# Causal scores in two row halves of the TensorE array, with the batch loop written out

## The chip, the cores and the metric

The kernel runs on one core of one Trainium2 chip. The metric is the device time of one execution in microseconds (us). A change of about 0.2% is what a measurement of this kernel can tell from none. TensorE (PE) does matmuls, VectorE (DVE) reductions and elementwise work, ScalarE (ACT) exponentials and copies, GpSimd (POOL) masks, and SyncE (SP) starts the DMAs.

## What is computed

Two layers over eight sequences of 512 tokens with 128 channels. The change lies in one part of the last layer, grouped-query causal attention with 16 heads of 8 channels and 4 key/value heads:

```python
q = (x @ wq.T).reshape(B, S, N_HEADS, HEAD_DIM)
k = (x @ wk.T).reshape(B, S, N_KV_HEADS, HEAD_DIM)
v = (x @ wv.T).reshape(B, S, N_KV_HEADS, HEAD_DIM)
attn = jnp.einsum('bqhd,bkhd->bhqk', q, k) * scale
attn = jnp.where(causal, attn, -jnp.inf)
attn = jax.nn.softmax(attn, axis=-1)
out = jnp.einsum('bhqk,bkhd->bqhd', attn, v).reshape(B, S, C)
return out @ wo.T
```

Here B = 8, S = 512, N_HEADS = 16, HEAD_DIM = 8. Before it stand dilated attention, a ternary feed-forward layer and a gated attention; behind it a mixture of eight experts.

## The kernel before

Five phases follow each other, each closed by a barrier of all engines; names in the profile begin with a_, b_, c_, d_ and e_ by phase. The change touches the end of c_ (projections) and all of d_ (`causal_attention_phase`).

**Precision by stacking.** Queries and keys are fp32 values held as three bf16 parts. Six products of parts are stacked along the contraction, so that one head's scores contract over 6 x 8 = 48 rows (`ROWS`) in one bf16 matmul. Phase c_ stores these stacks in `q_stack` and `k_stack` (L832, L834) with one entry for each batch, and an entry for a batch 8 that does not exist, since the loop of d_ loads one batch too many.

**Two heads in one layout.** `Qs` holds head i of the first eight heads on rows 0 to 47 and head 8 + i on rows 48 to 95. `Ks` has a slot for each key head, with the key on the 48 rows of its own half and zeros on the other 48 (L1173), so that a matmul over 96 rows gives the score of one head alone. Six more rows hold the negated row maxima of both heads (three bf16 parts each) against rows of ones and zeros (L1174 to L1184).

**First scores** (`first`, tile `pS`): for a head, query tile q against keys 0 to 128(q+1), 512, 384, 256 and 128 wide, and behind each a 128 x 128 matmul of the identity with the triangle of -1e30. These are three fills (f = 0: 512; f = 1: 384; f = 2: 256 and 128), in two PSUM buffers by turns. DVE takes the maxima of each (`maxima`, L1197 to L1200). They are split into three parts, transposed (`rows`, tile `pM`) and sent by DMA into the last rows of `Qs`.

**Second scores** (`second`, tile `pT`): keys by queries, for head i and head 8 + i together, now over 102 rows with the maximum subtracted; widths 512, 384, then 256 and 128 in three units. ACT takes the exponential of a unit into `P` (L1276), POOL cuts the diagonal blocks (L1167).

**Values** (`values`, tile `pO`): fp32 matmuls over 128 keys, four heads in four groups of 32 columns of the array at once. `by_token` transposes the result into `pM`, DVE divides.

**Order.** I call the work on one pair of heads a round: three units, eight rounds a batch, 64 in all. PE's queue in a unit is the second scores of the batch at hand, two fills of first scores of a pair three rounds ahead, and one step of the values of earlier heads. The first 22 heads' fills stand alone ahead of the first round; I call this the lead-in. The batches run as 0, a hardware loop over (1, 2), (3, 4), (5, 6), and 7; in the loop, waits go through registers. Batch 7 has no fills; batch 6 still makes those of six heads of the batch that does not exist. A matmul's rows in the profile are written rows*columns: 96*128 is 96 rows of contraction by 128 columns of weights.

Of the kernel before, what the change touches and what calls it, by code (L numbers as in the profile page):

```python
# [17 lines left out]
DH, HEADS = 64, 16  # L18
# [17 lines left out]


def wait_alone(eng, sem, count, unit=1):


    if not isinstance(count, int):
        count = eng.to_reg(count)
        eng.wait_ge(sem, unit)
    eng.wait_ge(sem, count)
# [749 lines left out]
def projection_phase(nc, top, dram):  # L794

    with ExitStack() as ctx:
# [22 lines left out]
        with nc.Block() as block:  # L819

            @block.sync
            def _(sp):
                for k in range(CHUNKS):
# [4 lines left out]
                    for b in (0, 1, 1) if k == CHUNKS - 1 else (0, 1):  # L828
                        entry = 2 * k + b + (1 if n_stored[c] == 12 * (k // 2) + 12 else 0)
# [184 lines left out]
def causal_attention_phase(nc, top, dram):  # L1014
# [11 lines left out]
    with ExitStack() as ctx:  # L1026
        ph = Phase(nc, ctx, "d_")
        sm = ph.sems("zeros ones ones_from max_ones S S_max part1 rest1 part2 rest2 parts mT_psum mT ST P masked PV O_sb O_T rden O_tok")
# [6 lines left out]
        Ks = [ph.sb(f"Ks{c}", [128, KV4, S], BF16) for c in two]  # L1035
# [16 lines left out]
        ALL_ROWS = 2 * ROWS  # L1052
        WITH_MAX = ALL_ROWS + 6
# [3 lines left out]
        def wait(eng, sem, value):  # L1057

            if not isinstance(value, int) or value > 0:
                eng.wait_ge(sem, value)  # L1060

        def steps(eng, step):
# [12 lines left out]
        def others(n, m, c, ahead):  # L1075

            return (n + 1, m + c, 1 - c) if ahead == 1 else (n + 2, m + 1, c)

# [6 lines left out]
        def turns(n, pair, unit, at):  # L1085

            got = turn(pair, unit, at)
            ended = isinstance(n, int) and n == B
            if got is None or (got[0] == 0 and ended) or (got[0] == 1 and isinstance(n, int) and n == 0):
# [4 lines left out]
        everything = [(k, f) for k in range(HEADS) for f in range(3)]  # L1094
        SPLIT_AT = HEADS // 2 - LEAD
        parity = [0]

        def par(n):

            if isinstance(n, int):  # L1100
                parity[0] = n % 2
            else:
                parity[0] = 1 - parity[0]
            return parity[0]

        with nc.Block() as block:

            @block.sync
            def _(sp):
                def load_stack(b, c, u):  # L1110

                    for a in two:
                        rows = slice(ROWS * a, ROWS * a + ROWS)
                        sp.dma_start(Qs[c][rows, 4 * u:4 * u + 4, :], dram["q_load"](b, 8 * a + 4 * u, 4))\
                            .then_inc(stacks[c][u], 16)
                        sp.dma_start(Ks[c][rows, 2 * a + u:2 * a + u + 1, :], dram["k_load"](b, 2 * a + u, 1))\
# [5 lines left out]
                def max_rows(n, m, c):  # L1122
# [4 lines left out]
                    for a in two:  # L1127
                        at = ALL_ROWS + 3 * a
# [3 lines left out]
                def step(n, m, more):  # L1132
                    c = par(n)
                    if more:
# [3 lines left out]
                        if not (isinstance(n, int) and n + 2 > B):  # L1138
# [4 lines left out]
                        sp.wait_ge(sm["ST"], n * NT + NT)  # L1143
                        load_stack(n + 2, c, 1)

                sp.wait_ge(sm["zeros"], 2)
# [5 lines left out]
                steps(sp, step)  # L1152

                for a in two:
                    sp.wait_ge(stacks[0][a], 64 * (B // 2 + 1))

            @block.gpsimd
            def _(pool):
                def step(n, m, more):
                    par(n)  # L1160
                    for pair in range(HEADS // 2):
                        for unit in range(3):

                            wait_alone(pool, sm["P"], n * NT + 3 * pair + unit + 1)
# [10 lines left out]
                for c in two:  # L1175

                    pool.wait_ge(sm["ones"], c + 1)
                    for a in two:
                        view = Ks[c][ALL_ROWS:128, 2 * a:2 * a + 2, :]
                        nc.gpsimd.affine_select(out=view, in_=view, compare_op=ALU.is_ge, fill=0.0, base=-3 * a,  # L1180
                                                pattern=[[0, 2], [0, S]], channel_multiplier=1)\
                            .then_inc(sm["ones_from"], 1)
                        pool.wait_ge(sm["ones_from"], 2 * c + a + 1)
                        nc.gpsimd.affine_select(out=view, in_=view, compare_op=ALU.is_ge, fill=0.0, base=3 * a + 2,  # L1184
                                                pattern=[[0, 2], [0, S]], channel_multiplier=-1)\
                            .then_inc(sm["max_ones"], 1)
                steps(pool, step)

            @block.vector
            def _(dve):  # L1190
                def maxima(n, c, some):
                    for k, f in some:
                        h, fill = ORDER[k], 3 * k + f
# [39 lines left out]
                def step(n, m, more):  # L1233
                    c = par(n)
                    for pair in range(HEADS // 2):
                        if more and pair == SPLIT_AT:
                            split(n + 1, 1 - c)
                        for unit in range(3):
                            if more:
                                for ahead, k, f in fills(pair)[2 * unit:2 * unit + 2]:  # L1240
# [553 lines left out]
```

## Time and profile before

| | us |
|---|---|
| time, median of 3 runs | 903.62 |
| lowest and highest | 902.7, 904.41 |
| profiled execution, first to last instruction (span) | 900.7 |
| median less span | 2.9 |
| PE, DVE, ACT busy in the span | 643.0, 559.2, 403.3 |
| first matmul of d_ | at 406.78 |
| first exponential of batch 0, of batch 7 | at 456.22, at 719.64 |
| last exponential ends | at 746.45 |

The execution's own time is not listed apart from its span, so the span is set against the median. The view by slices cuts the span into 40 pieces of 22.5 us; each digit is the busy share of an engine in tenths, and PEclk is the granted TensorE clock in tenths, so 5 is 1.2 GHz and 9 is 2.4 GHz but for a rest. PE's busy time in the views counts a matmul from start to end, and each overlaps the next; how fast PE goes is read from the distances between starts. The end of a row of several matmuls is the end of its last. In the views that group by form, the columns are busy time, mean ns of one, and the idle time of the engine before them.

### The profile page before, as it was taken

Reading aid. Unit: us, or ns where it says so; the run is one execution under the profiler, and the core shown is the slowest. Engines: PE = TensorE matmul, PEld = TensorE weight load, DVE = VectorE, ACT = ScalarE, POOL = GpSimd, SP = SyncE. Lnnn points to the kernel's source line nnn. Section 1 sums busy time; section 2 is a strip of 40 time slices with the busy share of each in tenths; the row PEclk is TensorE's granted clock in tenths of the full one; section 3 lists DMA queues with packets and bytes.
Section 4 is the critical chain, followed back from the end, with each engine's and each line's share of the span. In section 5 each row is a group of like instructions: output and inputs, shape, how many; then the busy total and the mean of one; then the engine's idle time right before and its main releaser. Section 6 shows DMA issues by size and latency. Waiting matters only on the chain. (4 is left out here: it accounts for less than half of the span.)

```text
span 900.7 us, 13426 instructions
## 1 busy us (share of the span) xinstructions
PE 643.0 (71%) x4232; PEld 372.4 (41%) x4232; DVE 559.2 (62%) x1764; ACT 403.3 (45%) x794; POOL 222.6 (25%) x340
## 2 busy tenths in 40 slices
PE   0816338938754480708899999999999996789651
PEld 0816328117644270403244445454444523555320
DVE  5786974042463535307878878788787801478897
ACT  3682565410203424400046566665665673456541
POOL 1040310010003032333023333333333341134344
PEclk9957655555965665755579999999999997799896
DMA  6000000000000050253001111111011100000001
GB/s 236 1 0 1 1 1 1 0 2 1 1 1 0 1 175 0 70 168 81 17 1 49 36 37 30 33 40 42 26 38 33 36 13 1 0 1 1 23 24 47
DMA packets 19369, 28.61 MB, mean 32 GB/s; under 512 B 3310, under 2 KB 15102, under 8 KB 19146
## 3 DMA queue, kind: packets, MB, share of 16 engines
q1 hardware_dynamic: 18746, 25.94, 9.5%
q10 hardware_dynamic: 576, 2.10, 0.6%
q8 instruction: 23, 0.38, 0.2%
q14 instruction: 24, 0.20, 0.1%
HBM read 14.57 MB, written 11.35 MB: 29 GB/s over the span
## 5 line engine op out<-in xcount | busy, mean ns | idle before, releaser
L1276 ACT ACTIVATE d_P<-d_pT 128x768 f32<-128x768 f32 (+1 forms) x192 | 167.9, 881 | 110.8 <-PE d_pT L1293 110.8
L1197 DVE TENSOR_REDUCE d_mx<-d_pS 128x1 f32<-128x512 f32 (+1 forms) x268 | 160.9, 620 | 66.2 <-PE d_pS L1293 61.5
L1293 PE MATMUL d_pS<-d_Ks,d_Qs 96*128 96x512 bf16 (+3 forms) x536 | 150.4, 329 | 31.2 <-DMA d_Ks<-k_stack 25.1
L1167 POOL TENSOR_SCALAR_AFFINE_SELECT d_P<-d_P 128x256 f32<-128x256 f32 x256 | 101.0, 406 | 233.5 <-ACT d_P L1276 233.4
L1293 PE MATMUL d_pS<-mask_bf,ident_bf 128*128 128x128 bf16 x536 | 111.4, 236 | 0.0
L1293 PE MATMUL d_pT<-d_Qs,d_Ks 102*128 102x512 bf16 (+3 forms) x512 | 103.7, 305 | 1.1 <-ACT d_P L1276 0.5
L1293 PE MATMUL d_pO<-d_P,d_V 128*32 128x512 f32 (+3 forms) x1024 | 96.5, 451 | 1.9 <-POOL d_P L1167 1.5
L1293 PEld LDWEIGHTS d_pS<-d_Ks,d_Qs 96*128 96x128 bf16 x536 | 54.2, 101 | 100.1 <-DVE d_mx L1197 32.8
L1623 PE MATMUL e_PE<-gate_expT,e_oT 128*128 128x512 f32 x128 | 62.5, 634 | 11.0 <-DVE e_T L1519 10.4
L421 PE MATMUL a_PS<-ident,N 128*128 128x128 f32 x96 | 21.5, 403 | 63.5 <-ACT N L320 51.6
L1199 DVE TENSOR_REDUCE d_mx<-d_pS 128x1 f32<-128x256 f32 x134 | 56.3, 420 | 13.5 <-PE d_pS L1293 11.1
L1293 PEld LDWEIGHTS d_pT<-d_Qs,d_Ks 102*128 102x128 bf16 x512 | 35.7, 99 | 69.1 <-ACT d_P L1276 49.5
L1450 POOL TENSOR_TENSOR e_T<-e_T 128x512 f32<-128x512 f32 x32 | 40.7, 1279 | 93.5 <-DVE e_T L1519 77.9
L1293 PEld LDWEIGHTS d_pS<-mask_bf,ident_bf 128*128 128x128 bf16 x536 | 55.5, 104 | 7.1 <-issue 0.3
L1605 ACT ACTIVATE e_T<-e_PE,e_comb 128x128 f32<-128x128 f32 x128 | 34.7, 383 | 45.0 <-PE e_PE L1623 19.6
L421 PEld LDWEIGHTS a_PS<-ident,N 128*128 128x128 f32 x96 | 17.8, 212 | 66.7 <-ACT N L320 54.6
L415 POOL TENSOR_TENSOR X<-X,a_nT 128x1024 f32<-128x1024 f32 x8 | 19.5, 2433 | 92.0 <-ACT a_nT L320 92.0
L1623 PEld LDWEIGHTS e_PE<-gate_expT,e_oT 128*128 128x128 f32 x128 | 24.7, 205 | 40.8 <-issue 23.3
L990 PE MATMUL c_PA<-ident,c_a 128*128 128x128 f32 x32 | 7.9, 428 | 46.6 <-ACT c_a L950 46.6
L320 ACT ACTIVATE N<-X,a_nb,a_rs 128x128 f32<-128x128 f32 x96 | 37.8, 479 | 1.1 <-DVE a_nb L161 0.8
L1200 DVE TENSOR_REDUCE d_mx<-d_pS 128x1 f32<-128x128 f32 x134 | 37.6, 281 | 0.0
L1258 ACT ACTIVATE d_mT<-d_pM 48x512 bf16<-48x512 bf16 x8 | 4.7, 590 | 65.3 <-PE d_pM L1364 65.2
(256 smaller groups left out, 1056.8 us busy)
## 6 DMA issues: line engine op xcount, KB each, us to landing
d_Qs<-q_stack SPq DMA_DIRECT2D x36, 192.0 KB, 2.9
q_stack<-c_Qp SPq DMA_DIRECT2D x9, 384.0 KB, 2.7
q_stack<-c_Qp SPq DMA_DIRECT2D x9, 256.0 KB, 3.0
X<-in_x_dram ACTq DMA_DIRECT2D x4, 512.0 KB, 7.7
d_V<-V SPq DMA_DIRECT2D x8, 256.0 KB, 2.3
out_dram<-e_moe SPq DMA_DIRECT2D x4, 512.0 KB, 2.6
d_Ks<-k_stack SPq DMA_DIRECT2D x36, 48.0 KB, 2.8
w_qkvT<-in_w_qkvT_dram SPq DMA_DIRECT2D x1, 1536.0 KB
```

Of the source, the lines that this page charges most:

```text
L320: last = nc.scalar.activation(dst(t), src(t), ACT.Identity, bias=nb[c][:, t:t + 1], scale=rs[c][:, t:t + 1])
L415: nc.gpsimd.tensor_tensor(X[c][:, :, :], X[c][:, :, :], y[c][:, :, :], ALU.add).then_inc(sm[s + "_x"], 1)
L421: last = nc.tensor.transpose(dst(t), src(t), ident)
L1167: last = nc.gpsimd.affine_select(out=view, in_=view, compare_op=ALU.is_ge, fill=0.0, base=0, pattern=[[0, 2], [1, 128]], channel_multiplie ...
L1197: last = nc.vector.reduce_max(mx[c][:, 3 - f, h:h + 1], src[:, 0:512 - 128 * f], AX.X)
L1199: nc.vector.reduce_max(mx[c][:, 1, h:h + 1], src[:, 0:256], AX.X)
L1200: last = nc.vector.reduce_max(mx[c][:, 0, h:h + 1], src[:, 256:384], AX.X)
L1276: nc.scalar.activation(P[pair % 4][:, :, P_AT[unit]:P_AT[unit] + w], pT[(3 * pair + unit) % 2][:, :, 0:w], ACT.Exp, scale=float(HD4) ** -0 ...
L1293: return nc.tensor.matmul(out, lhsT, rhs, start=start, stop=stop)
L1450: nc.gpsimd.tensor_tensor(T[u % 4][:, 0:NE // 2, :], T[u % 4][:, 0:NE // 2, :], T[u % 4][:, NE // 2:NE, :], ALU.add).then_inc(sm["halved"], 1)
L1605: last = nc.scalar.activation(T[u % 4][:, e, :], PE_[1][:, e, :], ACT.Copy, scale=comb[u // CT][:, u % CT, e:e + 1])
L1623: return nc.tensor.matmul(out_, lhsT, rhs, start=start, stop=stop)
```

## The change

Each head of a pair gets its own half of the array: head i on rows 0 to 47, its three maxima on 48 to 50, and head 8 + i on rows 64 to 111 and 112 to 114. `Ks` needs two slots for four, no zeros, and one fill with ones. First scores contract over 48 rows, second scores over 51, and the two heads' second scores stand next to each other, width by width. The triangle is still a matmul over 128 rows. Fills go pair by pair: both heads' 512, both 384, both 256 and 128. The loop is written out, so batch 8 is neither stored, loaded nor scored, and no wait goes through a register.

```diff
-                    for b in (0, 1, 1) if k == CHUNKS - 1 else (0, 1):
-                        entry = 2 * k + b + (1 if n_stored[c] == 12 * (k // 2) + 12 else 0)
+                    for b in two:
+                        entry = 2 * k + b
...
-        Ks = [ph.sb(f"Ks{c}", [128, KV4, S], BF16) for c in two]
+        Ks = [ph.sb(f"Ks{c}", [128, KV4 // 2, S], BF16) for c in two]
...
-        ALL_ROWS = 2 * ROWS
-        WITH_MAX = ALL_ROWS + 6
+        WITH_MAX = ROWS + 3
+        half = lambda a, n: slice(64 * a, 64 * a + n)
...
-            step(0, 0, True)
-            with eng.Fori(0, B // 2 - 1) as i:
-                step(2 * i + 1, i, True)
-                step(2 * i + 2, i + 1, True)
-            step(B - 1, B // 2 - 1, False)
+            for n in range(B):
+                step(n, n // 2, n % 2, n < B - 1)
...
-            return [(1 + k // HEADS, k % HEADS, f) for k in places for f in range(3)]
+            return [(1 + k // HEADS, k % HEADS, f) for f in range(3) for k in places]
...
+            return [(ahead, k, f) for ahead, k, f in fills(pair)[2 * unit:2 * unit + 2] if n + ahead < B]
...
-                sp.wait_ge(sm["zeros"], 2)
+                sp.wait_ge(sm["ones"], 2)
...
-                    nc.gpsimd.memset(Ks[c][0:ALL_ROWS, :, :], 0.0).then_inc(sm["zeros"], 1)
-                    nc.gpsimd.memset(Ks[c][ALL_ROWS:128, :, :], 1.0).then_inc(sm["ones"], 1)
...
+                    nc.gpsimd.memset(Ks[c][:, :, :], 1.0).then_inc(sm["ones"], 1)
...
-                            mm(dst[:, at:at + w], Qs[c][0:ALL_ROWS, i, 128 * q:128 * q + 128],
-                               Ks[c][0:ALL_ROWS, h // 4, 0:w], True, False)
+                            mm(dst[:, at:at + w], Qs[c][half(a, ROWS), i, 128 * q:128 * q + 128],
+                               Ks[c][half(a, ROWS), h // 4 % 2, 0:w], True, False)
                             last = mm(dst[:, at + w - 128:at + w], top.ident_bf[:, :], top.mask_bf[:, :],
                                       False, True)
...
-                    for j in two:
-                        for kt, at in ((0, 0),) if unit == 0 else ((1, 0),) if unit == 1 else ((2, 0), (3, 256)):
-                            w = S - 128 * kt
-                            last = mm(dst[:, j, at:at + w], Ks[c][0:WITH_MAX, 2 * j + pair // 4,
+                    for kt, at in ((0, 0),) if unit == 0 else ((1, 0),) if unit == 1 else ((2, 0), (3, 256)):
+                        w = S - 128 * kt
+                        for j in two:
+                            last = mm(dst[:, j, at:at + w], Ks[c][half(j, WITH_MAX), pair // 4,
                                                                   128 * kt:128 * kt + 128],
-                                      Qs[c][0:WITH_MAX, pair, 128 * kt:S])
+                                      Qs[c][half(j, WITH_MAX), pair, 128 * kt:S])
```

PE's queue in the lead-in, the first fills of the first pair of heads. Before:

```order
L1293 MATMUL d_pS0<-d_Ks0,d_Qs0 128x512
L1293 MATMUL d_pS0<-mask_bf,ident_bf 128x128
L1293 MATMUL d_pS1<-d_Ks0,d_Qs0 128x384
L1293 MATMUL d_pS1<-mask_bf,ident_bf 128x128
L1293 MATMUL d_pS0<-d_Ks0,d_Qs0 128x256
```

The same place after the change:

```order
L1255 MATMUL d_pS0<-d_Ks0,d_Qs0 128x512
L1255 MATMUL d_pS0<-mask_bf,ident_bf 128x128
L1255 MATMUL d_pS1<-d_Ks0,d_Qs0 128x512
L1255 MATMUL d_pS1<-mask_bf,ident_bf 128x128
L1255 MATMUL d_pS0<-d_Ks0,d_Qs0 128x384
```

The second head's 512 has moved up to stand behind the first head's, with the triangle still between them.

PE's queue in the rounds, the unit with the 256- and 128-wide second scores, up to the values that follow. Before:

```order
L1293 MATMUL d_pT0<-d_Qs1,d_Ks1 128x256
L1293 MATMUL d_pT0<-d_Qs1,d_Ks1 128x128
L1293 MATMUL d_pT0<-d_Qs1,d_Ks1 128x256
L1293 MATMUL d_pT0<-d_Qs1,d_Ks1 128x128
L1060 REGISTER_ALU
L1293 MATMUL d_pS0<-d_Ks0,d_Qs0 128x384
L1293 MATMUL d_pS0<-mask_bf,ident_bf 128x128
L1060 REGISTER_ALU
L1293 MATMUL d_pS1<-d_Ks0,d_Qs0 128x256
L1293 MATMUL d_pS1<-mask_bf,ident_bf 128x128
L1293 MATMUL d_pS1<-d_Ks0,d_Qs0 128x128
L1293 MATMUL d_pS1<-mask_bf,ident_bf 128x128
```

The same unit after the change:

```order
L1255 MATMUL d_pT0<-d_Qs0,d_Ks0 128x256 x2
L1255 MATMUL d_pT0<-d_Qs0,d_Ks0 128x128 x2
L1255 MATMUL d_pS0<-d_Ks1,d_Qs1 128x256
L1255 MATMUL d_pS0<-mask_bf,ident_bf 128x128
L1255 MATMUL d_pS0<-d_Ks1,d_Qs1 128x128
L1255 MATMUL d_pS0<-mask_bf,ident_bf 128x128
L1255 MATMUL d_pS1<-d_Ks1,d_Qs1 128x256
L1255 MATMUL d_pS1<-mask_bf,ident_bf 128x128
L1255 MATMUL d_pS1<-d_Ks1,d_Qs1 128x128
L1255 MATMUL d_pS1<-mask_bf,ident_bf 128x128
```

Equal widths of both heads now follow each other in the second scores, and this unit takes both heads' narrow fills, while the 384 has moved to the unit before it.

## Rows read from the trace of the kernel before

**Rows 1.** Page, 40 slices of the span: PE's busy tenths and its granted clock.
```profile
PE   0816338938754480708899999999999996789651
PEclk9957655555965665755579999999999997799896
```

**Rows 2.** Busy time of each engine in stretches (start:end, length, engines, granted clock).
```profile
core 0: us, PE busy (x) PEld busy (x) DVE busy (x) ACT busy (x) POOL busy (x), PEclk, DMA share, GB/s
158.64:171.40 12.76, 12.76 (x16) 2.12 (x16) 0.00 (x0) 7.01 (x7) 0.00 (x0) 0.50 0.00 0
328.00:334.00 6.00, 6.00 (x38) 6.00 (x39) 2.17 (x15) 0.00 (x0) 0.00 (x0) 0.50 0.94 277
406.78:455.12 48.34, 42.24 (x180) 15.13 (x181) 39.83 (x90) 1.87 (x2) 5.82 (x6) 0.50 0.17 38
455.12:460.60 5.48, 5.48 (x27) 3.14 (x26) 3.75 (x10) 2.64 (x3) 1.01 (x3) 0.50 0.00 0
568.96:606.52 37.56, 37.38 (x342) 18.39 (x340) 30.32 (x80) 23.55 (x29) 12.21 (x32) 1.00 0.12 34
719.64:746.45 26.81, 24.69 (x210) 8.28 (x208) 2.60 (x13) 21.83 (x28) 12.46 (x32) 1.00 0.07 19
```

**Rows 3.** Waits of batch 3, 568.96 to 606.52: total, times, longest.
```profile
PEld d_pS L1293 <- DVE d_mx L1197: 2.6, 10, 0.4
```

**Rows 4.** Timeline of PE in a round: start, length, operation, count.
```profile
600.82 0.22 PE L1293 MATMUL d_pS<-d_Ks,d_Qs 96*128 96x128 bf16 x1
600.87 0.22 PE L1293 MATMUL d_pS<-mask_bf,ident_bf 128*128 128x128 bf16 x1
601.02 0.85 PE L1293 MATMUL d_pO<-d_P,d_V 128*32 128x384 f32 x8
...
602.25 0.38 PE L1293 MATMUL d_pS<-d_Ks,d_Qs 96*128 96x512 bf16 x1
602.47 0.22 PE L1293 MATMUL d_pS<-mask_bf,ident_bf 128*128 128x128 bf16 x1
```

**Rows 5.** Groups by form: fp32 transposes of d_, one by one.
```profile
L1354 PE MATMUL d_pM<-ident,d_OT 128*128 128x128 f32 x128 | 19.6, 276 | 1.3 <-ACT d_OT L1265 1.3
```

**Rows 6.** Timeline of PE: 64-row matmuls in alternating halves of the array.
```profile
240.37 3.84 PE L701 MATMUL b_P<-b_QK 64*128 64x128 f32 x64 [0.89 <-DVE b_dY L633]
```

**Rows 7.** Timeline of PE: 128-row matmuls, then 8-row ones.
```profile
261.95 1.16 PE L701 MATMUL b_P<-w_outT,b_OT 128*128 128x128 f32 x6
263.04 0.48 PE L701 MATMUL b_P<-b_dY,batch_rows 8*128 8x128 f32 x2
263.37 0.38 PE L701 MATMUL b_P<-b_yu,batch_rows 8*128 8x128 f32 x2
```

**Rows 8.** Timeline of PE at clock 0.50: with and without a change of shape.
```profile
442.14 0.62 PE L1364 MATMUL d_pM<-ident_bf,d_m 128*48 128x128 bf16 x4 [1.70 <-DVE d_m L1215]
442.69 0.61 PE L1293 MATMUL d_pS<-d_Ks,d_Qs 96*128 96x512 bf16 x1
443.09 0.31 PE L1293 MATMUL d_pS<-mask_bf,ident_bf 128*128 128x128 bf16 x1
...
455.97 0.63 PE L1293 MATMUL d_pS<-d_Ks,d_Qs 96*128 96x512 bf16 x1
456.40 0.31 PE L1293 MATMUL d_pS<-mask_bf,ident_bf 128*128 128x128 bf16 x1
```

**Rows 9.** Timeline of all engines from the last stores of c_ to d_'s first matmul.
```profile
390.88 0.44 SPq L832 DMA_DIRECT2D q_stack<-c_Qp  x1
...
393.76 0.44 SPq L834 DMA_DIRECT2D k_stack<-c_Kp  x1
396.86 1.80 POOL L1173 MEMSET d_Ks<- 96x2048 bf16 x1 [14.33 <-POOLq L66]
...
402.39 0.34 SPq L1114 DMA_DIRECT2D d_Qs<-q_stack  x1
...
406.78 0.61 PE L1293 MATMUL d_pS<-d_Ks,d_Qs 96*128 96x512 bf16 x1 [25.09 <-DMA d_Ks<-k_stack]
```

More of the change, by code:

```diff
@@ L1093, in causal_attention_phase @@
         LAST_TURNS = [(u // 3, u % 3) for u in range(7)]
-        everything = [(k, f) for k in range(HEADS) for f in range(3)]
+        everything = [(k + j, f) for k in range(0, HEADS, 2) for f in range(3) for j in two]
+        fill_of = lambda k, f: 6 * (k // 2) + 2 * f + k % 2
         SPLIT_AT = HEADS // 2 - LEAD
[L1096 to L1104, printed above, removed]
         with nc.Block() as block:
@@ L1112, in load_stack @@
                     for a in two:
-                        rows = slice(ROWS * a, ROWS * a + ROWS)
-                        sp.dma_start(Qs[c][rows, 4 * u:4 * u + 4, :], dram["q_load"](b, 8 * a + 4 * u, 4))\
+                        sp.dma_start(Qs[c][half(a, ROWS), 4 * u:4 * u + 4, :], dram["q_load"](b, 8 * a + 4 * u, 4))\
                             .then_inc(stacks[c][u], 16)
-                        sp.dma_start(Ks[c][rows, 2 * a + u:2 * a + u + 1, :], dram["k_load"](b, 2 * a + u, 1))\
+                        sp.dma_start(Ks[c][half(a, ROWS), u:u + 1, :], dram["k_load"](b, 2 * a + u, 1))\
                             .then_inc(stacks[c][u], 16)
@@ L1137, in step @@
                         load_v(n + 1, 1 - c)
-                        if not (isinstance(n, int) and n + 2 > B):
+                        if n + 2 < B:
                             sp.wait_ge(sm["ST"], n * NT + NT // 2)
@@ L1151, in _, with step @@
                 max_rows(0, 0, 0)
-                steps(sp, step)
-                for a in two:
-                    sp.wait_ge(stacks[0][a], 64 * (B // 2 + 1))
+                steps(step)
             @block.gpsimd
             def _(pool):
-                def step(n, m, more):
-                    par(n)
+                def step(n, m, c, more):
                     for pair in range(HEADS // 2):
                         for unit in range(3):
-                            wait_alone(pool, sm["P"], n * NT + 3 * pair + unit + 1)
+                            pool.wait_ge(sm["P"], n * NT + 3 * pair + unit + 1)
                             for at in ((P_AT[0],), (P_AT[1],), P_AT[2:])[unit]:
@@ L1172, in _ @@
                 for c in two:
-                    nc.gpsimd.memset(Ks[c][0:ALL_ROWS, :, :], 0.0).then_inc(sm["zeros"], 1)
-                    nc.gpsimd.memset(Ks[c][ALL_ROWS:128, :, :], 1.0).then_inc(sm["ones"], 1)
[L1175 to L1187, printed above, removed]
+                    nc.gpsimd.memset(Ks[c][:, :, :], 1.0).then_inc(sm["ones"], 1)
+                steps(step)
             @block.vector
@@ L1192, in maxima @@
                     for k, f in some:
-                        h, fill = ORDER[k], 3 * k + f
+                        h, fill = ORDER[k], fill_of(k, f)
                         dve.wait_ge(sm["S"], n * NS + fill + 1)
@@ L1231, in divide, with step @@
                     last.then_inc(sm["O_tok"], 1)
[L1233 to L1234 removed]
+                def step(n, m, c, more):
                     for pair in range(HEADS // 2):
@@ L1239, in step @@
                             if more:
-                                for ahead, k, f in fills(pair)[2 * unit:2 * unit + 2]:
+                                for ahead, k, f in fills_of(n, pair, unit):
                                     b, _, b_c = others(n, m, c, ahead)
@@ L1358, in rows @@
                 def rows(n, c):
-                    if not (isinstance(n, int) and n == 0):
-                        wait_alone(pe, sm["O_tok"], (n - 1) * NG + 1)
-                    wait_alone(pe, sm["parts"], n + 1)
+                    wait(pe, sm["O_tok"], (n - 1) * NG + 1)
+                    pe.wait_ge(sm["parts"], n + 1)
                     for q in range(QT):
@@ L1373, in step @@
                             if more:
-                                for ahead, k, f in fills(pair)[2 * unit:2 * unit + 2]:
+                                for ahead, k, f in fills_of(n, pair, unit):
                                     first(*others(n, m, c, ahead), [(k, f)])
```

48 lines of the change are left out of this document (20 added, 28 removed).

## Prediction

> **What bounds the kernel now.** I read the slices first. PE is 90% busy or more from 20th to 34th slice, at clock 9, which is phase d_ from its first round on; in the slices before, of the lead-in, the clock is 5 [rows 1]. Then the stretches. A batch in the middle takes 37.56 us, of which PE is busy 37.38, DVE 30.32 and ACT 23.55: PE bounds the seven batches that have fills, and DVE is next, 7.2 us behind. Batch 7, without fills, takes 26.81 us, PE 24.69, ACT 21.83. The lead-in takes 48.34 us, DVE 39.83, PE 42.24 at 1.2 GHz; there PE and DVE wait for each other over two buffers [rows 2]. In the middle batch PE's weight loads stand only 2.6 us behind DVE's maxima [rows 3]. So a gain must take time out of PE's queue in the rounds, and whatever is added to that queue counts whole.
>
> Does the busy time hold stops? By widths a round has 2560 columns for the heads' first scores (2 x 1280), 1024 for the triangles (8 x 128), 2560 for the second scores, 2560 for the values (1280 x 4 fp32 passes, four column groups at once, for two rounds) and 512 for the transposes: 9216 columns, 3.84 us at 2.4 GHz. A round takes 37.56 / 8 = 4.70. The difference shows in the timeline: 128-wide matmuls in a row start 0.05 apart (600.82, 600.87), but behind the last one the values, in 32-column groups, start 0.15 later [rows 4]. PE stops for about 0.1 us when it goes from one shape of the array to another. A round has four such changes, 0.44 us; 0.42 is left for 3 to 5 ns a matmul and the waits for DVE.
>
> **What the change gives.** (1) Second scores. Whether two halves of the array work at once, phase b_ shows: 64 matmuls of 64 rows, in alternating halves, take 3.84 us. One lasts 0.27 to 0.28 [rows 5], so they start (3.84 - 0.27) / 63 = 57 ns apart [rows 6]. Two matmuls of this width in one and the same part of the array start 0.38 - 0.27 = 0.11 apart [rows 7]. So two heads run in the time of one: 1280 columns less, 0.53 us less 4 starts of 5 ns, 0.51 a round.
>
> (2) Start of d_. SP's first load waits for three memsets from 396.86 to 402.39, 5.53 us, and PE's first matmul for the load [rows 9]. Two memsets of half the width remain; at half of 1.80 each that is 1.85: 3.7 us earlier. If they took 1.80 each, 1.9.
>
> (3) Six stores less. Of the last 18 stores of c_, the last six run from 390.88 to 393.76 + 0.44 = 394.20 [rows 9], and d_ starts behind them: 3.3 us, at worst 0 if a transfer ends last.
>
> (4) Batch 8's six heads. Three rounds lose their fills: from 4.70 to 26.81 / 8 = 3.35, 4.0 us together. The loop's register waits stand in the trace as 0.4 us a turn at most: 1 us. Sum of 2 to 4: 12 us. The loads for batch 8 run beside all this and give nothing.
>
> **What it costs.** (5) Changes of shape. A 48-row matmul sits in half of the rows, the triangle in all of them. The nearest row: from 128-row to 8-row matmuls. The last of six 128-row ones starts at 261.95 + 1.16 - 0.27 = 262.84, the 8-row one at 263.04, 0.20 later for 0.11; to 263.37 there are 0.33 for two of 0.11, so its fp32 weights show as well [rows 7]. For bf16 weights at 1.2 GHz: the last 48-column transpose starts at 442.14 + 0.62 - 0.31 = 442.45, the 96-row one at 442.69, 0.24 for 0.11; but the next starts 0.40 later where 0.43 is usual: 0.11 net [rows 8]. I take 0.11 for each change, at either clock; ends 0.09 and 0.14. Counted in the new queue, a round has 18 changes for 4: six between matmul and triangle in its first two units, seven in the third, one more where second scores follow a triangle or a transpose. That is 14 x 0.11 = 1.54 us a round against 0.51 gained. Should shape by rows cost nothing, it is 0.
>
> The Trainium skill, TensorEngine Tiling (Array Packing), under Key Properties, says that changing the tiling mode drains TensorE, while changing the tile within a mode does not. [Rows 6, 7] agree with both halves of it. Its Performance Considerations promise up to 2x for a contraction of 64 or less, which here holds for the second scores alone.
>
> (6) Lead-in, eleven pairs of heads at 1.2 GHz. A pair takes PE 3584 columns, 2.99 us, of 48.34 / 11 = 4.39 with the transposes; 16 changes add 1.76. PE had up to 1.2 to spare, so the bounds are 0.5 and 1.8. A buffer's cycle (fill, maxima, next fill) is lengthened by the changes in its own fill only, 0.22, 0.22 and 0.44: 0.9 a pair, 10 us.
>
> (7) The clock, the largest term. The rounds are at 2.4 GHz because the clock rose at 460.6. Before that, for 5.48 us, 96-, 102- and 128-row matmuls stood back to back (PE busy 5.48 of 5.48); in the lead-in, the same 96-row matmuls with short stops between fills stayed at 1.2 GHz for all of 48 us. Matmuls over few rows stay there even without a stop: the 64-row ones from 158.64 to 171.40 (12.76 of 12.76 busy, clock 0.50), the 32-row ones from 328 to 334 [rows 2]. The new rounds begin at 1.2 GHz, with 48-row matmuls for a third of their columns and a stop at 18 places a round. That is like the lead-in and not like 455 to 460. So I take it that rounds with fills stay at 1.2 GHz. Their columns are 9216 - 1280 = 7936, 6.61 us; with 18 x 0.11 = 1.98 a round takes 8.6 us, far over DVE's 3.8 and ACT's 2.9. Against 4.70 that is +3.9, times 64 - 8 - 3 = 53 rounds: +207 us. The eleven rounds without fills are almost all long matmuls over 102 and 128 rows; there the clock should rise, 1 us late.
>
> Sum: -12 + 10 + 207 + 1 = +206; 903.6 + 206 = **1110 us**. (Profiled span 900.7 + 206 = 1107, and the 2.9 around it.) With 0.09 or 0.14 for a change, 18 x 53 of them give -19 or +29: its own range is 1088 to 1142.
>
> **Rivals.**
> - *The clock is full.* PE never pauses for microseconds in the new rounds, and batch 7 keeps its 1.00 with PE waiting now and then [rows 2]. Then a round is 4.70 - 0.51 + 1.54 less about 0.1 of waits that vanish = 5.6, +0.9 x 53 = +48; with -12 and +10: 950 us. The Trainium skill, TensorE: Matmul & The Clock Gate, says that sustained activity releases the clock and idle gaps bring the throttle back; by that rule it would be this case. The lead-in, 42 of 48 us busy and never released, speaks against it.
> - *Now one, now the other.* Values are long 128-row streams and could lift the clock at times, the fills let it fall. Half of the 53 rounds at each: about 1030 us.
> - *Faster.* The stop at a change between 48 and 128 rows is the term that decides: under 0.51 / 14 = 0.036 us the rounds get shorter, if the clock rises too. At nothing, a round is 4.70 - 0.51 = 4.2 (DVE allows 3.8): -27, with -12: 865 us. For it: no row shows exactly this pair of shapes. Against: a stop stands at every other pair of shapes that the trace shows [rows 4, 7, 8].
> - *It does not do what it says.* If 48 rows are run as a whole array, nothing overlaps and nothing stops: only the 12 us stay, 892, if the clock rises.
>
> **Numbers.** Stays at 1.2 GHz 0.60; part of the time 0.17; full clock 0.15; free changes 0.05; whole array 0.03. Faster than 903.6 by over 0.2% (what a measurement can tell from none) is 0.08, the last two; within 0.2% 0.01; slower 0.91. The range takes the first three cases: from 950 less 10 to 1142. It is wide because the clock decides it; the likeliest case alone is 1088 to 1142.
>
> **What would show it.** Right: PEclk 5 through the rounds and 9 only near the end of d_; a middle batch of 69 us, PE busy, DVE under half; two heads' second scores starting within 10 ns; the matmul behind a triangle starting 0.22 us after it (0.11 + 0.11), where 0.06 was [rows 4]; first matmul of d_ 7 us earlier. Wrong: a middle batch of 45 us says that the clock term failed; one of 34 us that the stops did; second scores 0.2 apart that the halves do not overlap. Lead-in near 48 us would say that its stops hide behind DVE.

## The result, and the profile after

The changed kernel takes 1111.1 us (median, 1110.1 to 1113.91), the kernel before 903.16 beside it: 1.2315 times as long, 95% interval 1.2262 to 1.2369. 1110 was predicted.

The slices of the profiled execution (span 1108.4 us, slices of 27.7 us), against [rows 1]:

```profile
PE   1553397676282559999999999999999998778762
...
PEclk9857555596565655555555555555555558879897
```

PE is busy as before, but the clock digit is 5 through the rounds, up to the 33rd slice, where it was 9 from the 22nd slice on. Stretches of the changed kernel, with the columns of [rows 2]: the lead-in, batch 0, a middle batch, batch 6 and batch 7.

```profile
core 0: us, PE busy (x) PEld busy (x) DVE busy (x) ACT busy (x) POOL busy (x), PEclk, DMA share, GB/s
399.43:456.40 56.97, 54.55 (x178) 18.32 (x178) 41.16 (x90) 1.87 (x2) 0.00 (x0) 0.50 0.15 31
457.55:521.39 63.84, 63.84 (x301) 19.35 (x300) 32.02 (x75) 23.23 (x29) 12.69 (x32) 0.50 0.06 15
662.23:732.65 70.42, 70.42 (x341) 21.25 (x340) 33.26 (x81) 23.71 (x30) 12.69 (x32) 0.50 0.08 20
873.49:928.50 55.01, 53.94 (x296) 16.61 (x295) 22.08 (x57) 22.91 (x30) 11.92 (x30) 0.57 0.04 11
928.50:955.44 26.94, 22.49 (x208) 6.63 (x206) 2.46 (x12) 21.53 (x29) 12.68 (x32) 0.94 0.01 2
```

The middle batch takes 70.42 us, a round 8.80, where it took 37.56 and 4.70. PE never pauses in it, DVE works under half of the time, and the clock is 0.50 throughout. In batch 6 the fills end, and there the clock rises (mean 0.57). Batch 7 is as long as before, 26.94 against 26.81. The waits have changed too. In [rows 3] PE's weight loads waited 2.6 us for DVE, and DVE waited 6.2 us for PE in the same batch; now no wait of PE for DVE is left in the middle batch, and DVE waits 34.9 us for PE (total, times, longest):

```profile
DVE d_mx L1163 <- PE d_pS L1255: 19.2, 16, 2.6
...
DVE d_mx L1161 <- PE d_pS L1255: 15.7, 16, 2.0
```

The timeline of PE in a round of the changed kernel answers to [rows 4, 8]; its columns are start, length, operation, count:

```profile
690.24 0.61 PE L1255 MATMUL d_pS<-d_Ks,d_Qs 48*128 48x512 bf16 x1
690.78 0.29 PE L1255 MATMUL d_pS<-mask_bf,ident_bf 128*128 128x128 bf16 x1
691.00 1.08 PE L1255 MATMUL d_pO<-d_P,d_V 128*32 128x256 f32 x8
692.01 0.50 PE L1255 MATMUL d_pT<-d_Qs,d_Ks 51*128 51x384 bf16 x2
692.30 0.52 PE L1255 MATMUL d_pS<-d_Ks,d_Qs 48*128 48x384 bf16 x1
692.76 0.29 PE L1255 MATMUL d_pS<-mask_bf,ident_bf 128*128 128x128 bf16 x1
692.98 0.50 PE L1255 MATMUL d_pS<-d_Ks,d_Qs 48*128 48x384 bf16 x1
```

At 1.2 GHz 512 columns take 0.43 us, and the triangle starts 0.54 behind them (690.24 to 690.78): 0.11 for the change of shape. Behind the triangle (0.11 for its columns) the next matmul starts 0.22 later, twice (690.78 to 691.00, 692.76 to 692.98): 0.11 again. And the two heads' second scores do run at once: they start 3 ns apart, 384 columns of one take 0.32 us, and the next matmul, of the same shape, starts 0.29 after them (692.01 to 692.30), where one after the other would be 0.64. Both mechanisms of the change are there, at their predicted prices; the clock is what makes 70 us of them.

The start of d_ in the changed kernel, against [rows 9]:

```profile
392.79 1.84 POOL L1150 MEMSET d_Ks<- 128x1024 bf16 x2 [10.40 <-POOLq L57]
394.65 0.32 SPq L1095 DMA_DIRECT2D d_Qs<-q_stack  x1
...
399.43 0.60 PE L1255 MATMUL d_pS<-d_Ks,d_Qs 48*128 48x512 bf16 x1 [17.87 <-DMA d_Ks<-k_stack]
```

**Where 207.7 us of span come from**, by the first exponential of each batch and the last one's end: first matmul of d_ 7.4 earlier (406.78 to 399.43); from there to the first exponential of batch 0, 8.7 more (49.44 to 58.12); from there to batch 7's, 207.5 more (263.42 to 470.95); batch 7, 0.1 more; the rest behind it, 1.3 less.

### The profile page after: what moved, and what is told of

Same layout as the page of the kernel before. It is cut to its first block and busy times, and to the rows that moved or that the text cites. A ratio compares the mean times of both kernels' runs of the same rounds, so it can differ in the third digit from the quotient of the medians.

```text
span 1108.4 us, 11828 instructions
## 1 busy us (share of the span) xinstructions
PE 861.7 (78%) x4184; PEld 387.4 (35%) x4184; DVE 569.8 (51%) x1740; ACT 403.8 (36%) x794; POOL 209.4 (19%) x330
## 2 busy tenths in 40 slices
DMA packets 17812, 26.81 MB, mean 24 GB/s; under 512 B 3086, under 2 KB 13726, under 8 KB 17578
## 5 line engine op out<-in xcount | busy, mean ns | idle before, releaser
L1255 PE MATMUL d_pS<-d_Ks,d_Qs 48*128 48x512 bf16 (+3 forms) x512 | 232.2, 454 | 18.6 <-DMA d_Ks<-k_stack 17.9
L1255 PE MATMUL d_pO<-d_P,d_V 128*32 128x512 f32 (+3 forms) x1024 | 153.1, 689 | 3.4 <-POOL d_P L1144 2.9
L1255 PE MATMUL d_pS<-mask_bf,ident_bf 128*128 128x128 bf16 x512 | 148.0, 289 | 0.0
L1255 PE MATMUL d_pT<-d_Qs,d_Ks 51*128 51x512 bf16 (+3 forms) x512 | 97.7, 429 | 1.8 <-ACT d_P L1238 1.5
L1255 PEld LDWEIGHTS d_pS<-d_Ks,d_Qs 48*128 48x128 bf16 x512 | 55.6, 109 | 64.7 <-DMA d_Ks<-k_stack 18.0
L1255 PEld LDWEIGHTS d_pT<-d_Qs,d_Ks 51*128 51x128 bf16 x512 | 21.6, 102 | 133.8 <-issue 120.8
L1255 PEld LDWEIGHTS d_pO<-d_P,d_V 128*32 128x32 f32 x1024 | 25.3, 135 | 21.9 <-issue 6.4
```

What stands on the lines that cost most here:

```text
L1255: return nc.tensor.matmul(out, lhsT, rhs, start=start, stop=stop)
```

## The experiments

My theory: few rows and many changes of shape together hold the clock down, and the clock is nearly all of the loss. The rivals: the rows alone do it; the changes alone do it; or the loss is the stops themselves. Times are medians of the kernel where a ratio stands with them; the six kernels without a ratio were executed once each. The kernel before took 900.96 in the median beside the first four, 902.6 beside the zeros over 48 rows and beside both gains together, and 902.5 beside the other four. Its single executions lie between 889.06 and 908.2 us, so a difference of 10 us between two single times shows nothing; small gains are read from the trace.

### The loop written out alone

The kernel before without batch 8: no stores, loads or fills for it, no register waits. Scores as before.

```diff
-            with eng.Fori(0, B // 2 - 1) as i:
-                step(2 * i + 1, i, True)
-                step(2 * i + 2, i + 1, True)
+            for n in range(B):
+                step(n, n // 2, n < B - 1)
```

> The kernel before with its batch loop written out, and nothing for batch 8 stored, loaded or scored; layout, zeros, fill order and 96-row first scores stay. My theory: only the small terms move: six stores 3.3 us, three rounds without fills 4.0, register waits 1: 903 - 8 = 895 us, clock 1.00 in the rounds, a middle batch 37.5 us. Rival (the dead work hides behind other things, or the longer program costs fetching): 903 or more. Second rival (the written-out loop itself keeps the clock down): over 1050.

Measured: 892.81 us, ratio 0.9933 (0.9896 to 0.997). Stretches, the lead-in, a middle batch, batches 6 and 7:

```profile
404.96:453.40 48.44, 42.37 (x181) 15.28 (x182) 39.93 (x90) 1.88 (x2) 5.61 (x6) 0.50 0.16 38
565.52:603.06 37.54, 37.36 (x341) 18.48 (x340) 30.37 (x81) 23.57 (x30) 12.62 (x33) 1.00 0.14 38
678.12:712.01 33.89, 32.95 (x296) 15.06 (x294) 20.43 (x57) 22.96 (x29) 12.44 (x32) 1.00 0.08 25
712.01:739.17 27.16, 24.65 (x208) 8.05 (x206) 2.46 (x12) 21.86 (x29) 12.62 (x32) 1.00 0.01 2
```

The middle batch is that of [rows 2]; the first matmul of d_ is 1.8 us earlier. From the first exponential to the last one's end the gain is 5.5 us (290.23 to 284.77), where 4 and 1 were predicted: 3.7 in batch 6, 1.0 in batches 1 to 5, and 1.1 in batch 0, where the clock rises 1.5 us after the first exponential and not 4.3; batch 7 gives 0.3 back. This part of the change is good, and cannot be blamed for anything.

### Changes of shape without few rows

The unrolled kernel before, scores over 96 and 102 rows, but the triangle over 64 rows: 18 changes of shape a round for 4. Half of the triangle's rows are left out, so 1024 of the 9216 columns of a round do run over fewer rows than before.

```diff
-   last = mm(dst[:, at + w - 128:at + w], top.ident_bf[:, :], top.mask_bf[:, :],
+   last = mm(dst[:, at + w - 128:at + w], top.ident_bf[0:64, :], top.mask_bf[0:64, :],
```

> The kernel before with its loop written out, but the triangle contracts over 64 rows (half of it is left out), so that each stands between two changes of shape, while first scores stay at 96 rows and second scores at 102, one after the other. Stops without the 48-row matmuls. Theory A (few rows keep the clock down): the clock rises in the rounds, a round 4.7 + 14 x 0.11 - 0.1 = 6.1 us, near 980 us. Theory B (the stops do): PEclk 5, a round 9216 columns at 1.2 GHz = 7.7 + 2.0 = 9.7 us, near 1165 us.

Measured: 1006.47 us. Its slices and three of its batches:

```profile
PE   0737088486736451889999999999999998688761
...
PEclk9957555559657565555555799999999999789896
```

```profile
464.76:537.28 72.52, 72.52 (x301) 24.02 (x300) 31.72 (x74) 23.54 (x29) 12.63 (x32) 0.50 0.05 14
537.28:595.86 58.58, 58.58 (x341) 22.86 (x340) 31.93 (x80) 23.68 (x29) 12.45 (x32) 0.77 0.07 20
643.34:690.82 47.48, 47.48 (x341) 20.68 (x340) 31.38 (x81) 23.57 (x29) 12.63 (x33) 1.00 0.10 29
```

The clock stays at 1.2 GHz for 100 us of rounds, rises at 564.6 us and then stays up. At full clock a round is 47.48 / 8 = 5.94 against 37.54 / 8 = 4.69: 1.24 us for 14 changes, 0.09 each, so the stops themselves cost 10 us a batch. They also delay the clock, but don't keep it down for good. The theory of the rows had 980; the other 26 us come mostly from these 100 us at the lower clock and from a lead-in that is 11 us longer.

### Few rows without changes of shape

The changed kernel with the triangle over 64 rows in the head's own half, so that fills have no change of shape; 5 changes are left in a round. Half of the triangle's rows are left out.

```diff
-   last = mm(dst[:, at + w - 128:at + w], top.ident_bf[:, :], top.mask_bf[:, :],
-             False, True)
+   last = mm(dst[:, at + w - 128:at + w], top.ident_bf[half(a, 64), :],
+             top.mask_bf[half(a, 64), :], False, True)
```

> The changed kernel, but the triangle contracts over 64 rows in the same half as its head, so a head has only half of its triangle (the other 64 queries of each diagonal block stay unmasked for the maxima). No change of shape is left between a first score and its triangle: 4 to 5 a round for 18. Matmuls over few rows stay. Theory A (few rows keep the clock down): PEclk 5 in the rounds, a round about 7936 columns at 1.2 GHz = 6.6 + 0.5 = 7.1 us less what the halves overlap, near 1020 us. Theory B (the stops keep it down): PEclk 9 in the rounds, a round 4.2 us, near 870 us. In either, 13 stops of 0.11 us less a round show what a change costs.

Measured: 887.28 us. Its fastest and its slowest full batch:

```profile
485.21:520.47 35.26, 33.05 (x340) 13.62 (x340) 30.19 (x81) 23.14 (x30) 12.62 (x32) 1.00 0.15 40
...
596.52:637.36 40.84, 38.40 (x340) 14.52 (x340) 30.85 (x81) 23.13 (x31) 12.62 (x32) 0.83 0.12 34
```

At full clock a batch takes 35.26 us, 2.3 less than before: the halves give what the change was made for. But the clock falls for some microseconds again and again, and a batch with such falls takes up to 5.6 us more (0.83). The theory of the stops had 870 for the kernel and counted neither the falls nor pauses of PE. PE also pauses in this kernel, for DVE and ACT, 2.2 us in the fastest batch, for 0.2 in [rows 2]. The stretch just before the fall at 548.0 us:

```profile
544.24:547.98 3.74, 2.96 (x34) 1.35 (x34) 3.02 (x8) 2.90 (x5) 0.95 (x3) 1.00 0.05 13
```

The other falls in the rounds of this kernel, of the next one and of the one with two scores and two triangles stand behind such pauses as well, and PE has none in the low stretch before a rise. So the falls may be the work of the pauses as much as of the rows; no run here separates the two. In the changed kernel and in the two with added zeros PE never pauses in the rounds with fills, so this rival does not touch them.

### The whole triangle as two 64-row matmuls

As the last, but with the full result: the triangle's 128 rows are copied once into the upper and the lower half (`tri`), and each head adds them by two 64-row matmuls in its own half, 128 and 64 columns wide.

```diff
-   last = mm(dst[:, at + w - 128:at + w], top.ident_bf[:, :], top.mask_bf[:, :],
-             False, True)
+   for part in two:
+       last = mm(dst[:, at + w - 128 + 64 * part:at + w], tri[half(a, 64), part, 0:128],
+                 tri[half(a, 64), part, 128 + 64 * part:256], False, part == 1)
```

> The changed kernel with the whole triangle, made of two 64-row matmuls (128 and 64 wide) in the half of its head: no change of shape between a first score and its triangle, 512 columns more a round, all of the result. Theory A (few rows keep the clock down): PEclk 5, a round 8448 columns at 1.2 GHz = 7.0 + 0.5 us less the overlap of the two heads, near 7.2: about 1030 us. Theory B (the stops do): PEclk 9, a round 4.70 - 0.51 + 0.21 less the overlap = 4.3, DVE next at 3.8: about 875 us, faster than the kernel before.

Measured: 900.82 us, ratio 1.0068 (1.0003 to 1.0133). Two batches:

```profile
492.14:528.78 36.64, 34.24 (x404) 17.62 (x404) 30.21 (x82) 23.16 (x30) 12.62 (x32) 1.00 0.14 38
528.78:570.73 41.95, 39.60 (x404) 19.11 (x404) 30.77 (x82) 23.16 (x31) 12.62 (x32) 0.84 0.12 33
```

Without the 13 changes of shape between scores and triangles the changed kernel is 210 us faster, although it does more matmuls. It is 26 us over the 875 of the theory of the stops, since the clock falls and PE pauses. A batch gains 0.9 us on the kernel before at full clock and loses 4.4 where the clock falls, so nothing is left over.

### Two scores, then two triangles

The changed kernel with both heads' first scores side by side and then both triangles: 8 changes a round for 18, nothing left out.

```diff
-   mm(dst[:, at:at + w], Qs[c][half(a, ROWS), i, 128 * q:128 * q + 128],
-      Ks[c][half(a, ROWS), h // 4 % 2, 0:w], True, False)
-   last = mm(dst[:, at + w - 128:at + w], ...)
+   for a in two:
+       ...
+       mm(pS[a][:, at:at + w], Qs[c][half(a, ROWS), h % 8, 128 * q:128 * q + 128],
+          Ks[c][half(a, ROWS), h // 4 % 2, 0:w], at == 0, False)
+   for a in two:
+       for q, at in parts:
+           last = mm(pS[a][:, at + w - 128:at + w], ...)
```

> The kernel after, with the fills of a pair of heads written as both heads' scores side by side and then both triangles: 8 changes of shape a round for 18, and the first scores of two heads at once; rows and result as in the kernel after. Theory A, few rows and some stops are enough to hold the clock down: rounds at 1.2 GHz, 8.8 less 10 changes of 0.12 and less 1280 columns (1.07 us): 6.5 us, a middle batch of 52 us, about 990 us. Theory B, the stops decide: the clock rises at least for a part of the time, as it did without any stop at the triangle; at full clock a round is 4.4 or more with the waits for DVE (both buffers are filled at once): 35 to 43 us a batch, 890 to 940 us.

Measured: 975.96 us, between the two. Two batches:

```profile
563.44:610.87 47.43, 43.42 (x340) 15.62 (x340) 30.52 (x81) 23.54 (x30) 12.63 (x33) 0.86 0.10 29
610.87:658.95 48.08, 44.49 (x340) 15.89 (x340) 30.51 (x81) 23.55 (x30) 12.63 (x33) 0.82 0.11 30
```

The clock goes up and down within every batch (0.82 to 0.86), and PE has pauses of 4 us in a batch besides, since both buffers are now filled at once and DVE empties them one by one. Neither of my two numbers was right. At 48 rows the clock is low always with 18 changes a round, now and then with 8, and now and then with the 5 of the two kernels above; the last two groups also have PE's pauses.

### More work over 128 rows, the same changes

The changed kernel plus a matmul of the identity with zeros between each first score and its triangle, as wide as the score: 2560 columns more a round, all over 128 rows; 18 changes as before; nothing left out.

```diff
+   mm(dst[:, at:at + w], top.ident_bf[:, :], nothing[:, 0:w], False, False)
    last = mm(dst[:, at + w - 128:at + w], top.ident_bf[:, :], top.mask_bf[:, :],
```

> The kernel after, and in each first score, between it and its triangle, one matmul more: the identity over all 128 rows with zeros, as wide as the score (2560 columns more a round, nothing left out of the result). The clock stays at 1.2 GHz in the kernel after because few of its columns run over many rows and 18 changes of shape a round stop PE. Theory A, the rows: with the zeros most columns run over 128 rows, the number of changes is the same, and the clock rises to 2.4 GHz in the rounds: 5.6 + 2560 columns at 2.4 GHz, 1.07 = 6.7 us a round, a middle batch of 54 us, about 1006 us, faster than the kernel after although it does more. Theory B, the stops decide alone: the clock stays at 0.50, a round takes 8.8 + 2.13 = 10.9 us, a middle batch 87 us, about 1225 us.

Measured: 1019.46 us, 92 less than the changed kernel, with more work. Slices, and a stretch at the begin of batch 0 and a middle batch:

```profile
PE   0736089495717362999999999999999998688761
...
PEclk9957555568657575555699999999999999689896
```

```profile
479.82:502.50 22.68, 22.68 (x91) 5.56 (x90) 10.04 (x21) 7.12 (x8) 3.97 (x10) 0.50 0.00 1
588.81:640.47 51.66, 51.66 (x405) 18.85 (x404) 32.65 (x81) 23.58 (x29) 12.62 (x32) 1.00 0.10 27
```

The clock rises at 502.5 us, 23 us into the rounds, and stays. The lead-in costs 21 us more, which my 1006 had not counted. The timeline of PE shows what a change costs at full clock:

```profile
611.06 0.22 PE L1257 MATMUL d_pS<-mask_bf,ident_bf 128*128 128x128 bf16 x1
611.21 0.33 PE L1257 MATMUL d_pS<-d_Ks,d_Qs 48*128 48x384 bf16 x1
611.48 0.34 PE L1257 MATMUL d_pS<-d_nothing,ident_bf 128*128 128x384 bf16 x1
611.65 0.22 PE L1257 MATMUL d_pS<-mask_bf,ident_bf 128*128 128x128 bf16 x1
```

Behind the 48-row matmul of 384 columns (0.16 us) the next starts 0.27 later, behind the 128-row one of the same width 0.17: 0.10 for the change. Behind the triangle (0.05) it is 0.15: 0.10. So a change costs about 0.10 at 2.4 GHz and 0.11 at 1.2 GHz; it does not scale with the clock.

### The same work over 48 rows

As the last, with the added matmul over the 48 rows of the head's own half: the same columns, the same 18 changes, the same zeros.

```diff
-   mm(dst[:, at:at + w], top.ident_bf[:, :], nothing[:, 0:w], False, False)
+   mm(dst[:, at:at + w], Qs[c][half(a, ROWS), i, 128 * q:128 * q + 128],
+      nothing[half(a, ROWS), 0:w], False, False)
```

> As the run with zeros over 128 rows (1019.46 us, clock 1.00 in the rounds from 555 us on), but the added matmul runs over the 48 rows of the head's own half of the array: the same 2560 columns more a round, the same 18 changes of shape, the same busy time of PE; only the number of rows of the added work differs. Theory A, the rows of the work count: the clock stays at 0.50 while there are fills, a round takes 8.80 + 2.13 = 10.9 us, a middle batch 87 us, about 1225 us. Theory B, more work between two stops is what raised the clock: it rises again, a middle batch 51.7 us, about 1020 us.

Measured: 1245.75 us. A middle batch:

```profile
647.41:734.90 87.49, 87.49 (x405) 25.51 (x404) 33.23 (x81) 23.71 (x30) 12.68 (x32) 0.50 0.06 17
```

87.49 us where 87 was expected; the total is 20 more than I had, since the lead-in is longer here too (first exponential at 479.0, not 457.6). The two kernels differ in one matmul and by 226 us. With equal columns, changes of shape and share of busy time, the clock rises with this matmul over 128 rows and not over 48. How busy PE was does not tell the two apart; it is 87.49 of 87.49 here, and 51.66 of 51.66 there. One difference goes along with the rows: the weights are the identity there and the head's queries here, both against zeros. No run has the identity over 48 rows, so the weights are not ruled out. Each is one execution, and they ran on different chips; the kernel before takes 902.5 and 902.6 beside them.

### Only the second scores in halves

The unrolled kernel before; second scores in two halves of 51 rows (a second layout `Kh` of the keys, with ones), first scores over 112 rows with zeros in the other head's half, no change of shape to the triangle. The second scores now stand between two changes, so a round has 8 for 4.

```diff
-   mm(dst[:, at:at + w], Qs[c][0:ALL_ROWS, i, 128 * q:128 * q + 128],
-      Ks[c][0:ALL_ROWS, h // 4, 0:w], True, False)
+   mm(dst[:, at:at + w], Qs[c][0:112, i, 128 * q:128 * q + 128],
+      Ks[c][0:112, h // 4, 0:w], True, False)
...
+   for j in two:
+       last = mm(dst[:, j, at:at + w], Kh[c][half(j, WITH_MAX), pair // 4, ...],
+                 Qs[c][half(j, WITH_MAX), pair, 128 * kt:S])
```

> The kernel before with the loop written out, and only the second scores in two halves of the array (51 rows each, two heads at once); the first scores stay over all rows (112, with zeros in the other head's half) and the triangle behind them has no change of shape. Theory A, the overlap is worth 0.51 us a round and a change of shape 0.10: a round of 4.69 - 0.51 + 4 x 0.10 = 4.6 us, a middle batch of 36.7 us, granted clock 1.00 in the rounds (few changes, more than half of the columns over 112 or 128 rows), about 889 us. Theory B, the clock falls at times, as with all scores in halves: batches of 37 to 42 us, 890 to 920 us. Theory C, the overlap is worth nothing: a batch of 40.8 us, 915 us.

Measured: 888.3 us. A middle batch, and PE's timeline in it:

```profile
562.17:598.97 36.80, 36.37 (x341) 15.28 (x340) 30.43 (x81) 23.48 (x30) 12.63 (x33) 1.00 0.17 44
```

```profile
579.90 0.39 PE L1284 MATMUL d_pT<-d_Qs,d_Kh 51*128 51x512 bf16 x2
580.22 0.39 PE L1284 MATMUL d_pS<-d_Ks,d_Qs 112*128 112x512 bf16 x1
580.45 0.22 PE L1284 MATMUL d_pS<-mask_bf,ident_bf 128*128 128x128 bf16 x1
```

Both heads' 512 columns and the change of shape behind them take 0.32 us (579.90 to 580.22), 0.21 for the columns and 0.10 for the change; one after the other the two alone would take 0.43. The clock holds at 1.00. A batch takes 36.80 against 37.54: 0.09 us a round, as 0.51 less the four added changes of 0.10 gives. The overlap is real, and pays about what the changes around it leave. With its 8 changes a round this kernel keeps the clock at 1.00, where the one with two scores and two triangles, also with 8, has 0.82 to 0.86: its first scores run over 112 rows and not 48, and PE pauses 0.4 us a batch and not 4.

### The first load behind one memset

The unrolled kernel before; batch 0's loads wait for the memset of their own buffer alone, not for both buffers'. The memsets with ones move behind both memsets with zeros.

```diff
-                sp.wait_ge(sm["zeros"], 2)
                 for b in two:
+                    sp.wait_ge(sm["zeros"], b + 1)
                     for u in two:
                         load_stack(b, b, u)
```

> The kernel before with the loop written out, and batch 0's load no longer waits for the memsets of the second buffer. The first load then starts behind one memset (1.8 us) and not three (5.5 us): the first matmul of d_ 3.7 us earlier, all else as with the loop written out alone: 889 us, ratio 0.985 to the kernel before. If the last stores of c_ end last instead, the gain is 0 to 2 us: 891 to 893 us.

Measured: 888.24 us, ratio 0.9807 (0.9668 to 0.9945). The first memset of d_ to the first matmul:

```profile
392.32 3.54 POOL L1169 MEMSET d_Ks<- 96x2048 bf16 x2 [10.29 <-POOLq L66]
394.15 0.32 SPq L1111 DMA_DIRECT2D d_Qs<-q_stack  x1
...
398.58 0.61 PE L1290 MATMUL d_pS<-d_Ks,d_Qs 96*128 96x512 bf16 x1 [17.38 <-DMA d_Ks<-k_stack]
```

6.3 us, where it was 9.9 in [rows 9]: the 3.7 of the prediction's second term. The interval of the ratio is wide (one of the four executions took 877.17), so the gain is read from these rows.

### Both gains together

Second scores in halves, and the loads behind their own buffer's memsets.

```diff
-                sp.wait_ge(sm["zeros"], 4)
-                sp.wait_ge(sm["q_zeros"], 2)
                 for b in two:
+                    sp.wait_ge(sm["zeros"], 2 * b + 2)
+                    sp.wait_ge(sm["q_zeros"], b + 1)
```

> The kernel before with the loop written out, the second scores in halves (first scores over all rows), and batch 0's loads behind the memsets of the first buffer alone. The two gains stand at different places and should add: a middle batch of 36.8 us, clock 1.00 in it, the first matmul of d_ at 399 us instead of 403.6; 888.3 less 3 to 4 = 885 us, ratio 0.981. If the added K loads or the memset of the queries end last, only 1 us is gained: 887 us.

Measured: 887.02 us, ratio 0.9882 (0.9809 to 0.9956). A middle batch is 36.80 us as expected. From the first memset to the first matmul it is 8.5 us (397.37 to 405.87), for 11.3 with the halves alone: 2.8 gained, not 3.7, since this layout has a second memset and a third load for each part. The times of this kernel and of the two before it, 887.0, 888.2 and 888.3, can't be told apart. By the ratios this one is 1.2% and the early load 1.9% below the kernel before, with intervals that end below 1. The kernel with second scores in halves alone was executed once, and the kernel before has come as low as 889.06; what shows its gain is the middle batch.

### Side by side

| kernel | rows of first scores, of what lies between them and the triangle's end | changes a round | middle batch, us | clock in it | us |
|---|---|---|---|---|---|
| before, unrolled | 96, 128 | 4 | 37.5 | 1.00 | 893 |
| second scores in halves | 112, 128 | 8 | 36.8 | 1.00 | 888 |
| changes without few rows | 96, 64 | 18 | 72.5, 58.6, then 47.5 | 0.50, then 1.00 | 1006 |
| half triangle in halves | 48, 64 | 5 | 35.3 to 40.8 | 1.00 to 0.83 | 887 |
| split triangle in halves | 48, 64 | 5 | 36.6 to 41.9 | 1.00 to 0.84 | 901 |
| two scores, two triangles | 48, 128 | 8 | 47.4 to 48.1 | 0.86 to 0.82 | 976 |
| after | 48, 128 | 18 | 70.4 | 0.50 | 1111 |
| after + zeros, 128 rows | 48, 128, 128 | 18 | 51.7 | 1.00 | 1019 |
| after + zeros, 48 rows | 48, 48, 128 | 18 | 87.5 | 0.50 | 1246 |

## Why the prediction was right

- **What bounds it** (PE in the rounds): right. The middle batch stretched with PE's queue alone, and DVE and ACT went on with the same work (30.3 to 33.3 and 23.6 to 23.7 us busy).
- **(1) Second scores, -0.51 a round**: right. 36.80 for 37.54 in the kernel that does this alone, with the four changes that it adds.
- **(2), (3) The start, -7.0**: -7.35 in the profile. From the memset to the first matmul it is 6.6 for 9.9 (-3.3 for -3.7). The last stores end 4.0 earlier, for 3.3; but in the other kernels without these six stores they end between 389.4 and 394.6 us, because the phases ahead of them vary by some us, so this term is not settled to better than 2 us.
- **(4) Batch 8 and register waits, -5**: -4.7 in batches 1 to 6 of the unrolled kernel; the rest of its -5.5 is the earlier rise of the clock in batch 0, less what batch 7 lost.
- **(5) 0.11 for a change of shape at either clock**: 0.11 at 1.2 GHz in the changed kernel, 0.09 to 0.10 at 2.4 GHz. The rows of weight loads of other types had given the right size.
- **(6) The lead-in, +10**: 8.7. A pair of heads takes 0.8 more, not 0.9; the reading that PE's slack hides about half of its 16 changes held (PE is now busy 54.55 of 56.97 us).
- **(7) The clock**: a round of 8.6 was predicted, 8.80 measured. 6.61 us of columns and 2.19 for 18 changes, 0.12 each with what else stands between matmuls; I had 0.11 and nothing else. Batches 1 to 5 are 163.4 longer where 155 was predicted, 8 more. Batch 0 is 26.7 longer where its eight rounds were counted at 31, since its first rounds have few values yet (63.84 us and not 70.42); this was not foreseen and takes half of it back. In all, the batches are 207.5 longer where +207, -5 and +1 were predicted, so 4.5 more. With 1.3 less in the lead-in and 1.3 less behind d_, the sum comes within 2 us of the result. The term was right in kind and size; a nearness of 1 us is luck, since errors of up to 8 us cancel.
- **The reason given for (7)** was two causes together, and a stretch of 64-row matmuls without any stop at 1.2 GHz as evidence that rows alone suffice [rows 2]. That evidence was weak. These matmuls use only 16 columns of weights besides, and the 64-row ones of [rows 6], over all 128 columns, run at a granted clock of 1.00. The first line is of the timeline, the second a stretch:

```profile
158.64 13.83 PE L425 MATMUL a_PS<-a_expS,w1T 64*16 64x512 f32 x16
...
240.37:244.21 3.84, 3.84 (x64) 3.65 (x64) 1.36 (x2) 1.18 (x2) 0.00 (x0) 1.00 0.02 4
```

The runs bear out that rows and stops both count, and correct the weights. The stops, with first scores over 96 rows, delay the rise by 100 us. Few rows with 5 changes a round let the clock rise soon and lose it at times, behind pauses of PE. Few rows with 18 changes never let it rise while there are fills, unless work over 128 rows is added. The added zeros show the rows' part with columns and changes equal, but for the weights used.
- **Slips that change nothing**: the slices at clock 9 are the 22nd to the 33rd [rows 1], not the 20th to the 34th. By its own -19 and +29 the likeliest case is 1091 to 1139, not 1088 to 1142; the 3 us at either end are not explained.
- **The rivals**: the sustained-activity case gave 950. By the Trainium skill, TensorE: Matmul & The Clock Gate, Part 1 (The HAM clock gate), the gate follows how busy PE has been; here the trace does not agree, with 70.42 of 70.42 us busy at 0.50. A clock that goes up and down, the mixed case, is what the kernel with two scores and two triangles shows, at 976 us. Free changes are refuted by 0.10; overlap that does not happen, by 0.29 for two matmuls of 0.32.

What stays open: why the clock rises just when it does in the two kernels in which it rises late (at 564.6 and at 502.5 us) and then never falls again, and whether the rows or PE's pauses set off the single falls in the kernels with 48-row fills. The table gives an order, not a rule by which one could work it out.

## What to carry to other kernels

Running two small contractions side by side saves columns, but every matmul of another shape between them costs about 0.1 us at either clock: count the changes in the queue, and do it only where the saved columns exceed them, as with second scores that stand together. Then ask what it does to the clock: a PE that is 100% busy with matmuls over few rows and with stops can sit at 1.2 GHz for a whole phase. Look in the trace of before for stretches like the new queue, in rows, columns of weights and stops, read their granted clock (here the lead-in, at 0.50 though 42 of 48 us busy), and price the change at both clocks.

## What the runs showed of the hardware

- Adding 2560 columns a round of multiplication by zeros over 128 rows made the kernel 92 us faster (1111 to 1019), and the same columns over 48 rows made it 135 us slower (1246).
- Two matmuls in different halves of the array take the time of one: two 51-row ones start 3 ns apart, and the matmul behind them starts 0.29 us later for 384 columns each at 1.2 GHz.
- The price of a change of shape between 48 and 128 rows hardly depends on the clock: 0.10 us at 2.4 GHz, 0.11 at 1.2.
- A clock that has risen late can hold: over 96 and 64 rows with 18 stops a round it was 0.50 for 100 us of rounds and 1.00 for the following 220, with PE busy without a pause in both.
